# The centring of an expert layer's down weights, its first table and its weight loads moved into the recurrence of a fused kernel

## The chip, the cores and the metric

One NeuronCore of a Trainium2 chip runs the whole program. The metric is the time of one execution in microseconds; less is better. The engines are PE (TensorE), DVE (VectorE), ACT (ScalarE), POOL (GpSimd) and SP (SyncE), which here only issues DMAs. All data are fp32.

## What is computed

`x` is 16 sequences of 512 tokens of 128 channels. A gated delta rule over 16 heads of 8 channels is followed by a residual and a layernorm; then a mixture of 8 experts (top 1) with SiLU gating, again with residual and layernorm.

```python
def step(S, inp):                       # per head, over 512 tokens
    k_t, q_t, v_t, beta_t, a_t = inp
    S = S * a_t[..., None, None]
    delta = (v_t - einsum('bhd,bhde->bhe', k_t, S)) * beta_t
    S = S + k_t[..., :, None] * delta[..., None, :]
    return (S, einsum('bhd,bhde->bhe', q_t, S))
ctx = rmsnorm(ys, norm_w) * silu(gate)          # then ctx @ Wo.T + bo
x = layernorm(x + attn(x))
e = argmax(router(x))                            # one expert a token
out = down_w[e] @ (silu(gate_w[e] @ x) * (up_w[e] @ x))
x = layernorm(x + out)
```

## The kernel before

The 512 tokens of a sequence are cut into 16 blocks (`NW`) of 32 tokens, all 16 sequences at once; a block is eight chunks (`NCH`) of four tokens. A body function per engine (`pe_body`, `act_body`, `pool_body`, `dve_body`, `sp_body`) is called for block -1 (start-up), 0 to 15 and 16 (the tail), and each engine keeps the order in which its body writes the instructions. In block w the recurrence runs on block w, the projections are made for w+2 (`a`), the K products for w+1 (`n`), the outputs y for w-1 (`p`), residual, attention output and first layernorm for w-2 (`o`), the routing for w-3. Semaphores order the engines: `b.step` names an instruction, `b.wait` waits for it.

DVE's body is written by chunk: `chunk(c)` issues the product with the state (L1862), the decayed state (L1873), the reduction (L1878), the mix (L1882), its reduction (L1888), the update (L1892) and its reduction into the new state (L1904). Behind L1878, L1882, L1888, L1892 and L1904 stand five slots, `between(c, 0)` to `between(c, 4)`, in which other work of the block is put by hand: the routing steps (`route_part` 0 to 9), `y_next` (L1583), the eight `y_n` steps (L1555), `kkd`, `qkd`, `q_norm`. A slot is named (c, k) below. L1873 of chunk 0 waits for POOL's `solve3` of the block; the y of block w-1 is stored by SP after `y_n7`.

SP's body is a queue too. Per block: stores and loads of z, beta, v, x, q; then `x_res` (after PE's residual), the y store, the K store, the y load (after the y store has landed), the K load (after the K store has landed) and the Q load. K is written to HBM and read back in another layout; POOL's products of the next block start with it. POOL's body holds, in order, the eight products `q_prod` of a block, the products `kk` and `qk`, the decays, `ctx`, `k_gam`, `k_end`, `q_gam`, the `u` and `solve` steps, and the indirect DMAs that send finished rows to the sorted table (three a block from block 4 on).

In block 15 (`b.last`) the order differs: `last_between` places the steps; SP loads gate, up and down weights there. The first table (`table_a`, steps 0 to 15, on one partition) says which expert each of the first 29 tiles of 128 sorted rows takes; it needs the counts of the first nine blocks (`WA`). Its temporaries lie in a PSUM bank (`side`). Steps 0 to 10 are in block 15, the others in the tail (`last_outputs`), as are the memsets `pads` and the centring of the down weights: `centre_down` takes the mean of each of 24 rows of 128 out of `down_we` so that the output of the experts has no mean. The expert stage then takes 71 tiles through PE, ACT and DVE (`expert_pe`, `expert_act`, `expert_dve`), the first steps of which lie between PE's, ACT's and DVE's last attention work.

SBUF before: the attention's buffers (`sa`) lie first, and `gate_up_we`, `down_we`, `w_tile` and what follows are laid over them after `att.close()`.

## Time and profile before

| | |
|---|---|
| runs, us | 773.49, 773.37, 770.83 (median 773.37) |
| the profiled execution, us | 774.71, its span 772.9 |
| busy: PE, DVE, POOL, ACT | 84%, 82%, 78%, 54% of the span |
| mean granted clock of TensorE | 0.925 |
| start-up, until the first chunk | 26.5 us |
| blocks 0 to 15 | 26.5 to 568 us |
| tail and experts | 568 to 772.9 us |

Times in the rows are us from the span's start. A timeline row has the start, the duration, the engine, the line and the tiles written and read; a bracket gives the idle time before it and what ended it. A row with x3 stands for three instructions merged, its duration from the start of the first to the end of the last. Most instructions of POOL have the line of a helper (L1311) and are told apart by their tiles.

### The profile page before, as it was taken

To read this page: it belongs to the slowest core of one execution; us is meant where nothing else is said; L and a number is where in the kernel's file an instruction comes from. 1 tells how busy PE (TensorE), PEld (TensorE's weight loads), DVE (VectorE), ACT (ScalarE), POOL (GpSimd) and SP (SyncE) were. 2 spreads that over 40 slices of the span, in tenths; PEclk is the share of its full clock that TensorE was granted. 3 is DMA by queue.
4 is the path that set the end of the run, shared out by engine and by line. 5 is a ranking of instruction groups with operands and counts; after the bars stand their busy time and mean duration, and the time that the engine had idled before them with its cause. 6 is when DMAs were issued, how large, how long until landed. Compare 5 with 4: busy or idle time off the path is not lost.

```text
span 772.9 us, 13851 instructions
## 1 busy us (share of the span) xinstructions
PE 651.5 (84%) x3513; PEld 499.5 (65%) x3513; DVE 632.9 (82%) x1701; ACT 416.5 (54%) x1313; POOL 601.4 (78%) x758
## 2 busy tenths in 40 slices
PE   8668698889989887897988999496879979999990
PEld 3435374747657464664747556384778979999990
DVE  3899999999999999999999999999892535666530
ACT  6736456565565665566566546432324446666651
POOL 2888787979999899999999999999561527444574
PEclk9989799899999999999999999789669999999996
DMA  6734243341625334262433515304534655776730
GB/s 175 199 100 99 47 121 84 85 124 51 157 60 131 96 91 106 73 157 70 126 93 89 122 51 136 88 22 159 195 106 138 205 215 175 254 245 232 233 118 9
DMA packets 135919, 97.28 MB, mean 126 GB/s; under 512 B 95630, under 2 KB 110225, under 8 KB 135714
## 3 DMA queue, kind: packets, MB, share of 16 engines
q1 hardware_dynamic: 130514, 87.55, 40.2%
q0 software_dynamic: 4320, 8.43, 3.3%
q8 instruction: 30, 0.49, 0.3%
q10 hardware_dynamic: 1008, 0.43, 0.2%
q14 instruction: 47, 0.39, 0.2%
HBM read 39.80 MB, written 31.43 MB: 92 GB/s over the span
## 4 chain that ended last, share of the span: by engine, by line
PE 33%; DVE 31%; POOL 19%; issue 7%; ACT 6%; DMA 2%; ACTq 0%; DVEq 0%; POOLq 0%; SPq 0%
PE banks L436 12%; DVE banks L1904 6%; PE banks L449 6%; DVE banks L1878 5%; POOL q_prod L1311 5%; DVE upd L1892 5%; DVE prod L1862 4%; DVE banks L1888 3%; DVE mix L1882 3%; PE banks L695 3%; POOL u L1311 3%; DVE upd L1873 3%; PE banks L849 2%; PE banks L676 1%; POOL kkqk L1311 1%
## 5 line engine op out<-in xcount | busy, mean ns | idle before, releaser
L1311 POOL TENSOR_TENSOR q_prod<-s_keep,q_gam 128x512 f32<-128x512 f32 x128 | 140.5, 1099 | 15.8 <-ACT d_keep L1012 8.6
L1008 ACT ACTIVATE s_keep<-banks 128x128 f32<-128x128 f32 x128 | 50.2, 392 | 179.2 <-DVE upd L1892 177.2
L752 PE MATMUL banks<-q_prod,ident 128*128 128x240 f32 (+1 forms) x496 | 112.6, 381 | 24.6 <-POOL q_prod L1311 24.6
L752 PEld LDWEIGHTS banks<-q_prod,ident 128*128 128x128 f32 x496 | 93.9, 194 | 44.9 <-POOL q_prod L1311 35.0
L1904 DVE TENSOR_REDUCE banks<-upd 128x128 f32<-128x640 f32 x128 | 105.8, 826 | 7.7 <-DVE upd L1892 0.5
L436 PE MATMUL banks<-xs_t,w_tile 128*128 128x128 f32 x852 | 108.9, 278 | 3.6 <-issue 2.7
L545 POOL DMA_INDIRECT out<-rows_out,xs x71 | 70.0, 986 | 51.5 <-ACT rows_out L526 43.4
L436 PEld LDWEIGHTS banks<-xs_t,w_tile 128*128 128x128 f32 x852 | 102.3, 194 | 4.8 <-issue 4.4
L580 DVE TENSOR_TENSOR hid<-banks,silu 128x384 f32<-128x384 f32 x71 | 39.6, 557 | 72.9 <-PE banks L436 42.2
L1878 DVE TENSOR_REDUCE banks<-prod 128x64 f32<-128x576 f32 x128 | 93.6, 732 | 0.0
L1862 DVE TENSOR_TENSOR prod<-banks,k_gam 128x512 f32<-128x512 f32 x128 | 88.3, 690 | 3.4
L1892 DVE TENSOR_TENSOR upd<-banks,k_end 128x512 f32<-128x512 f32 x128 | 88.4, 690 | 1.9
L349 POOL DMA_INDIRECT x_sorted<-x_all,place x64 | 63.5, 993 | 17.6 <-issue 10.2
L695 PE MATMUL banks<-kkqk,ident 128*128 128x256 f32 (+1 forms) x272 | 64.0, 392 | 7.7 <-DVE qkd L1573 3.6
L676 PE MATMUL banks<-x_ct,w_proj 128*128 128x512 f32 x128 | 66.0, 640 | 2.8 <-DMA x_ct<-in_x_ct 2.8
L695 PEld LDWEIGHTS banks<-kkqk,ident 128*128 128x128 f32 x272 | 51.4, 202 | 18.4 <-issue 6.2
L449 PE MATMUL banks<-down_we,hid 128*128 x426 | 60.6, 279 | 0.5 <-issue 0.2
L1888 DVE TENSOR_REDUCE banks<-mix 128x64 f32<-128x256 f32 x128 | 54.4, 425 | 1.3
L449 PEld LDWEIGHTS banks<-down_we,hid 128*128 128x128 f32 x426 | 53.7, 194 | 1.6 <-issue 1.5
L1882 DVE TENSOR_TENSOR mix<-solve,banks 128x256 f32<-128x256 f32 x128 | 53.7, 419 | 1.0
L1873 DVE TENSOR_TENSOR upd<-banks,decays 128x128 f32<-128x128 f32 x128 | 48.9, 382 | 0.1
L950 PE MATMUL banks<-x_ct,ident 128*128 128x512 f32 x78 | 41.4, 671 | 8.1 <-DVE y_n L1555 8.1
(224 smaller groups left out, 1454.9 us busy)
## 6 DMA issues: line engine op xcount, KB each, us to landing
w_tile<-gate_up_we SPq DMA_DIRECT2D x71, 352.0 KB, 3.1
xs<-x_sorted SPq DMA_DIRECT2D x71, 64.5 KB, 2.2
x_ct<-in_x_ct SPq DMA_DIRECT2D x16, 256.0 KB, 3.0
k_dram<-kq_s SPq DMA_DIRECT2D x16, 256.0 KB, 2.9
q_dram<-kq_s SPq DMA_DIRECT2D x16, 256.0 KB, 3.9
out<-v_s SPq DMA_DIRECT2D x16, 256.0 KB, 2.6
out<-beta SPq DMA_DIRECT2D x16, 256.0 KB, 3.4
k_h<-k_dram SPq DMA_DIRECT2D x16, 256.0 KB, 3.2
```

Of the source, the lines that this page charges most:

```text
L436: last = mm(ps(tile)[:, c * P:(c + 1) * P], w_tile[tile % NG][:, g * I + c * P:g * I + (c + 1) * P], xs_t[tile % NX][:, :], start=True, st ...
L449: last = mm(down_ps[tile % 2][:, 0:D], hid[tile % NH][:, c * P:(c + 1) * P], down_we[:, c, :, :].rearrange("p e d -> p (e d)")[:, bass.ds( ...
L676: b.step(label, win, lambda: mm(by_slot(bank), w_proj[:, m, :], x, start=True, stop=True))
L695: i = mm(out[:, first:last], ident[:, :], kkqk[:, d, first:last], start=(d == 0), stop=(d == DH - 1))
L752: i = mm(out, ident[:, :], q_prod[m][:, d, :, 1 - m:], start=(m == 0 and d == 0), stop=(d == DH - 1), skip_group_check=True)
L1311: b.step(label, win, lambda: tt(out, x, y, op))
L1862: v.tensor_tensor(pr[:, :, 0:DH].rearrange("p (e b j) d -> p e b j d", e=DH, b=2), s_in.unsqueeze(3).to_broadcast(wide), k_gam[par][:, c, ...
L1878: v.tensor_reduce(k_s, pr, AX, ALU.add).then_inc(s_read, 1)
L1882: v.tensor_tensor(mix[:, :, :, :], solve[par][:, c, :, :, :], k_s.rearrange("p (n j) -> p n j", j=C).unsqueeze(2).to_broadcast([P, DH * 2, ...
L1888: v.tensor_reduce(delta, mix[:, :, :, :], AX, ALU.add).then_inc(s_delta, 1)
L1892: v.tensor_tensor(upd[:, :, 0:C].rearrange("p (e b d) j -> p e b d j", e=DH, b=2), delta.rearrange("p (e b) j -> p e b j", b=2).unsqueeze( ...
L1904: v.tensor_reduce(after[:, 0:P], upd[:, :, :], AX, ALU.add).then_inc(s_state, 1)
```

## The change

- `down_we` gets a place of its own in SBUF and is loaded in block 4. ACT centres it, three of the 24 rows of 128 a block, in blocks 6 to 13: one pass that sums the scaled row, one that adds the negative mean. DVE's `centre_down` goes.
- The sixteen steps of the first table go to eight slots each of blocks 13 and 14, and their temporaries (`tab`) from PSUM to SBUF.
- Gate and up weights are loaded in block 14, at its start on SP, instead of in block 15.
- In block 15 the routing steps 5 to 9 come in chunks 5 to 7 instead of 3 to 5; the memsets of the weight tiles come in (5, 3).
- In blocks 1 to 14 the `y_n` steps start in (4, 4) instead of (4, 3), and the last two are in (7, 1) and (7, 3) instead of (6, 3) and (7, 1).
- On ACT `q_squares` comes behind the first `keep` and `fill` of a block instead of ahead of them.
- The SBUF plan is changed so that the new places are free when they are written.

```diff
         fill_at = sb("fill_at", [1, E], I32)
+        tab = sb("tab", [1, 4 * E + TA * (E + 2)])
+        down_we = sb("down_we", [P, IC, E, D])
+        down_neg, down_sc = sb("down_neg", [P, IC * E]), sb("down_sc", [P, D])
 
 
...
-
+        v_h, k_gam, k_end, solve, q_gam = {}, {}, {}, {}, {}
+
+        def of_block(n):
...
+        v_h[1], v_h[2] = (sa(f"v_h{n}", [P, DH * 2 * C, NCH]) for n in (1, 2))
+        v_h[0] = sa("v_h0", [P, DH * 2 * C, NCH])
         a_h = two_a("a_h", [P, 2, C, NCH])
         z_h = sa("z_h", [P, 2 * T])
...
-        down_we = sb("down_we", [P, IC, E, D])
...
-        s_wpad, s_wmean, s_wdown = sem("s_wpad"), sem("s_wmean"), sem("s_wdown")
+        s_wpad, s_wdown = sem("s_wpad"), sem("s_wdown")
...
             v = nc.vector
-            at = 64
-            counts, shifted, whole, ends = (side[0:1, at + n * E:at + (n + 1) * E] for n in range(4))
-            past = side[0:1, at + 4 * E:at + 4 * E + TA * E].rearrange("p (s e) -> p s e", e=E)
-            row, expert_ps = (side[0:1, at + 4 * E + TA * (E + n):at + 4 * E + TA * (E + n + 1)] for n in range(2))
+            counts, shifted, whole, ends = (tab[:, n * E:(n + 1) * E] for n in range(4))
+            past = tab[:, 4 * E:4 * E + TA * E].rearrange("p (s e) -> p s e", e=E)
+            row, expert_ps = (tab[:, 4 * E + TA * (E + n):4 * E + TA * (E + n + 1)] for n in range(2))
...
-                    eng.wait_ge(s_wmean, 3)
+                    eng.wait_ge(act.sem, act.at["centred23", CENTRE + IC * E // 3 - 1])
...
-            for n in range(NG):
-                v.memset(w_tile[n][:, 2 * I:I + IC * P], 0.0).then_inc(s_wpad, 1)
...
                 b.step("logits", win, lambda: A(logits[:, at:at + TW, :],
                                                 post_of(win)[:, 0:TW * E].rearrange("p (i e) -> p i e", i=TW), ACT.Copy))
 
+            def centre_down(j):
+
+                n = 3 * (w - CENTRE) + j
+                if not 0 <= n < IC * E:
+                    return
+                block = down_we[:, :, :, :].rearrange("p c e d -> p (c e) d")[:, n, :]
+                if n == 0:
+                    b.wait_dma(s_wdown, 1)
+                b.step(f"mean{n}", w, lambda: A(down_sc[:, :], block, ACT.Copy, scale=-1.0 / D, accum_out=down_neg[:, n:n + 1]))
+                b.wait(act, f"mean{n}", w)
+                b.step(f"centred{n}", w, lambda: A(block, block, ACT.Identity, bias=down_neg[:, n:n + 1]))
+
             def start_up():
 
                 b.wait(pe, "k", 0)
...
                     nc.scalar.preload_act_table_set("natural_log_exp_and_others")
             if b.pre:
                 decay_of(n)
-                q_squares(n)
             keep(NCH * w)
             if b.chain:
                 fill(4 * w + 1)
+            if b.pre:
+                q_squares(n)
             if b.load:
                 b.wait(pe, "v", a)
                 b.wait_dma(s_vst, a)
...
                 fill(4 * w + 2)
+            centre_down(0)
             if b.post:
                 y_square()
             keep(NCH * w + 3)
...
+            centre_down(1)
             if b.load:
                 softplus(a)
             keep(NCH * w + 6)
             fill(4 * w + 4)
+            centre_down(2)
             if b.out:
                 router_logits(o)
 
...
+                places = ((0, 3), (1, 0), (1, 1), (1, 2), (2, 1), (2, 2), (3, 3), (3, 4))
+                if w in (NW - 3, NW - 2) and (c, k) in places:
+                    table_a_part(len(places) * (w - NW + 3) + places.index((c, k)))
...
                     kkd_part(k + 1)
-                if b.post and c == 4 and 3 <= k:
-                    if k == 3:
-                        b.wait(act, "y_r1", p)
-                    y_n_part(k - 3)
+                if b.post and c == 4 and k == 4:
+                    b.wait(act, "y_r1", p)
+                    y_n_part(0)
                 if b.post and c == 5 and k < 4:
-                    y_n_part(k + 2)
+                    y_n_part(k + 1)
                 if b.pre and c == 5 and k == 4:
                     q_norm_part()
                 if b.pre and c == 6 and k < 3:
                     qkd_part(k)
                 if b.post and c == 6 and k == 3:
-                    y_n_part(6)
-                if b.post and c == 7 and k == 1:
-                    y_n_part(7)
+                    y_n_part(5)
+                if b.post and c == 7 and k in (1, 3):
+                    y_n_part(6 + k // 2)
 
             def last_between(c, k):
 
@@ -1757,24 +1771,26 @@
                     y_next_part()
                 if c == 2 and k < 2:
                     route_part(r, 3 + k)
-                if c == 3 and k < 3:
-                    route_part(r, 5 + k)
                 if c == 3 and 3 <= k:
                     if k == 3:
                         b.wait(act, "y_r1", p)
                     y_n_part(k - 3)
                 if c == 4 and k < 3:
                     y_n_part(2 + 2 * k, 2)
-                if c == 4 and k == 4:
+                if c == 5 and k < 3:
+                    route_part(r, 5 + k)
+                if c == 6 and k == 4:
                     route_part(r, 8)
-                if c == 5 and k == 0:
+                if c == 7 and k == 0:
                     route_part(r, 9)
-                if c == 5 and 1 <= k:
-                    table_a_part(k - 1)
-                if c == 6:
-                    table_a_part(4 + k)
-                if c == 7 and k < 2:
-                    table_a_part(9 + k)
+                if c == 5 and k == 3:
+                    pad_weights()
+
+            def pad_weights():
+
+                if not b.dry:
+                    for n in range(NG):
+                        nc.vector.memset(w_tile[n][:, 2 * I:I + IC * P], 0.0).then_inc(s_wpad, 1)
 
             def table_a_part(k):
 
...
                     q_end[:, :, :].rearrange("p d b -> p b d").unsqueeze(1).to_broadcast([P, DH, 2, DH]), ALU.mult))
                 if not b.dry:
-                    for k in range(11, n_table_a):
...
                     y_ps[p % 2].rearrange("p (n t) -> p n t", t=T)[:, :, T - 1], ends, AX, ALU.add))
-                if not b.dry:
-                    for k in range(n_table_a, n_steps_a):
-                        table_a(e, k)
-                    centre_down(e)
...
                 e.dma_start(x_res[:, :], t["x_ct"][:, p, :]).then_inc(s_xres, 16)
-                b.wait(pool, "solve3", w)
-                b.wait(pe, "kkqk", w)
-                for s in (s_kst, s_qst, s_vst, s_bst, s_zst):
-                    b.wait_dma(s, NW)
-                e.dma_start(gate_up_we[:, :, 0, :], t["gate_w"]).then_inc(s_wexp, 16)
-                e.dma_start(gate_up_we[:, :, 1, :], t["up_w"]).then_inc(s_wexp, 16)
...
                 q_store(a)
+            if w == CENTRE - 2:
+                e.dma_start(down_we[:, :, :, :], t["down_w"]).then_inc(s_wdown, 16)
+            if w == NW - 2:
+                b.wait(act, "silu", NW - 1)
+                b.wait(pe, "warm", NW - 3)
+                b.wait(pool, "ctx", NW - 5)
+                b.wait(pool, "k_n", NW - 1)
+                e.wait_ge(s_kst, 16 * NW)
+                e.wait_ge(s_qst, 16 * NW)
+                e.wait_ge(s_vst, 16 * NW)
+                e.wait_ge(s_bst, 16 * NW)
+                e.wait_ge(s_zst, 16 * NW)
+                e.dma_start(gate_up_we[:, :, 0, :], t["gate_w"]).then_inc(s_wexp, 16)
+                e.dma_start(gate_up_we[:, :, 1, :], t["up_w"]).then_inc(s_wexp, 16)
             if b.post:
                 b.wait(pe, "res", o)
                 e.dma_start(x_res[:, :], t["x_ct"][:, p, :]).then_inc(s_xres, 16)
```

## Rows read from the trace of the kernel before

**Rows 1.** Busy time by stretch: span, engines (instructions), granted clock, DMA share, GB/s.
```profile
397.70:431.20 33.50, 30.11 (x134) 20.23 (x133) 32.67 (x83) 20.00 (x61) 31.91 (x43) 0.95 0.41 102
...
531.80:568.10 36.30, 26.48 (x120) 23.63 (x120) 33.41 (x83) 11.74 (x52) 24.36 (x25) 0.76 0.53 181
...
583.80:772.90 189.10, 164.73 (x1409) 160.88 (x1409) 87.38 (x336) 100.83 (x370) 93.52 (x96) 0.95 0.56 186
```

**Rows 2.** Waits of DVE, 60 to 560 us: total, times, longest.
```profile
DVE banks L1614 <- PE banks L839: 2.1, 1, 2.1
...
DVE y_n L1555 <- ACT y_rms L1039: 1.6, 1, 1.6
...
DVE banks L1904 <- ACT d_keep L1012: 0.3, 1, 0.3
```

**Rows 3.** Timeline of DVE, ends and starts of blocks: start, us, instruction [idle before].
```profile
294.62 0.21 DVE L1555 TENSOR_TENSOR y_n<-banks,y_rms 128x64 f32<-128x64 f32 x1
...
295.20 0.69 DVE L1892 TENSOR_TENSOR upd<-banks,k_end 128x512 f32<-128x512 f32 x1
...
296.92 0.69 DVE L1862 TENSOR_TENSOR prod<-banks,k_gam 128x512 f32<-128x512 f32 x1
297.72 0.39 DVE L1873 TENSOR_TENSOR upd<-banks,decays 128x128 f32<-128x128 f32 x1
...
330.64 0.69 DVE L1862 TENSOR_TENSOR prod<-banks,k_gam 128x512 f32<-128x512 f32 x1
331.25 0.38 DVE L1873 TENSOR_TENSOR upd<-banks,decays 128x128 f32<-128x128 f32 x1
```

**Rows 4.** Timelines of SP, POOL, DVE, blocks 10 and 11; landing of `k_h`.
```profile
395.61 0.34 SPq L1923 DMA_DIRECT2D out<-y_n  x1
...
398.99 0.33 SPq L1983 DMA_DIRECT2D k_h<-k_dram  x1
...
402.36 2.10 POOL L1311 TENSOR_TENSOR kkqk<-k_h 128x384 f32<-128x384 f32 x3 [0.64 <-DMA k_h<-k_dram]
...
428.90 2.11 POOL L1311 TENSOR_TENSOR solve<-u,b_h 128x384 f32<-128x384 f32 x3
...
431.19 0.69 DVE L1862 TENSOR_TENSOR prod<-banks,k_gam 128x512 f32<-128x512 f32 x1
...
DMA to landing us min/median/max: 2.6/3.2/4.2
```

**Rows 5.** Timeline of DVE in block 15, without and with a table step.
```profile
537.54 0.42 DVE L1882 TENSOR_TENSOR mix<-solve,banks 128x256 f32<-128x256 f32 x1
538.00 0.43 DVE L1888 TENSOR_REDUCE banks<-mix 128x64 f32<-128x256 f32 x1
...
560.87 0.42 DVE L1882 TENSOR_TENSOR mix<-solve,banks 128x256 f32<-128x256 f32 x1
561.21 0.39 DVE L274 TENSOR_TENSOR banks<-banks,iota_t 1x232 f32<-1x232 f32 x1
561.52 0.40 DVE L1888 TENSOR_REDUCE banks<-mix 128x64 f32<-128x256 f32 x1
```

**Rows 6.** A POOL product, instructions of the tile `k_gam`: min/median/max ns.
```profile
L1311 POOL TENSOR_TENSOR k_gam<-k_h,decays x16: 1267/1278/1303, 20.7 to 511.0; 128x512 f32<-128x512 f32 x16
```

**Rows 7.** Timelines of PE and SP in block 15, end of the residual.
```profile
551.44 1.91 PE L783 MATMUL banks<-center,x_res 128*128 128x128 f32 x8
...
553.38 0.33 SPq L2027 DMA_DIRECT2D x_res<-in_x_ct  x1
553.82 0.38 SPq L1923 DMA_DIRECT2D out<-y_n  x1
```

**Rows 8.** Timeline of ACT in block 7: a Square with accumulation, and the next.
```profile
285.53 0.27 ACT L1096 ACTIVATE post_sq<-banks 128x128 f32<-128x128 f32 x1
...
285.78 0.28 ACT L1096 ACTIVATE post_sq<-banks 128x128 f32<-128x128 f32 x1
```

**Rows 9.** Timeline of DVE in the tail: the last y product.
```profile
582.24 0.69 DVE L1820 TENSOR_TENSOR y_n<-banks,y_rms 128x512 f32<-128x512 f32 x1 [2.73 <-ACT y_rms L1039]
```

More of the change, by code:

```diff
@@ L122, in two_a @@
             return [sa(f"{name}{n}", shape) for n in range(2)]
+        spare = sa("spare", [P, 1480])
         x_ct = two_a("x_ct", [P, WN])
@@ L128, in block_kernel @@
         v_s = sa("v_s", [P, WN])
+        gate = {n: sa(f"gate{n}", [P, WN]) for n in (1, 2)}
         k_h = two_a("k_h", [P, DH, 2, C, NCH])
@@ L138, in block_kernel @@
         z_relu, z_log = sa("z_relu", [P, 2 * T]), sa("z_log", [P, 2 * T])
-        v_h = [sa(f"v_h{n}", [P, DH * 2 * C, NCH]) for n in range(3)]
         decays = two_a("decays", [P, 2, 9, NCH])
-        k_gam = two_a("k_gam", [P, NCH, 2, C, DH])
-        k_end = two_a("k_end", [P, NCH, 2, DH, C])
-        solve = two_a("solve", [P, NCH, DH * 2, C, C])
+        of_block(1)
         kkd = sa("kkd", [P, 96])
@@ L149, in block_kernel @@
         x_res = sa("x_res", [P, WN])
-        gate = [sa(f"gate{n}", [P, WN]) for n in range(5)]
-        q_gam = two_a("q_gam", [P, NCH, DH, 2, C])
+        gate.update({n: sa(f"gate{n}", [P, WN]) for n in (0, 3, 4)})
         q_norm = [sa(f"q_norm{n}", [P, 2 * T]) for n in range(3)]
@@ L205, in block_kernel @@
         tail_top, tail_place = (side[:, n:n + TW] for n in (SIDE + 2 * TW * E, SIDE + 2 * TW * E + TW))
-        down_mean = side[:, SIDE + 80:SIDE + 80 + IC * E]
         cand, before = (chain_ps[n][:, 2 * P:2 * P + TW * E].rearrange("p (t e) -> p t e", e=E) for n in range(2))
```

18 lines of the change are left out of this document (6 added, 12 removed).

## The prediction

> **What bounds the kernel now.** I read the table of stretches first, by block. A block is eight chunks of the recurrence, each starting with the DVE product of L1862. In a typical block DVE is busy 32.7 of 33.5 us, POOL 31.9, ACT only 20.0 [rows 1]; block 15 takes 36.3 to its end. DVE's order is the clock of the first 568 us: DVE's waits from block 1 to block 15 come down to three, of 2.1 us (block 15), 1.6 and 0.3 (both block 3), beside small change [rows 2]. So anything that adds to DVE's order, or makes DVE wait, is paid in full; work on ACT is not, as long as it comes before it is needed. After 583.8 us TensorE works through the experts: 164.7 us busy in 189.1 [rows 1].
>
> The second thing to see is how near POOL is to being the bound. At each block's start DVE's second instruction (L1873) needs POOL's last step for that block, `solve3`. Its natural place is 0.61 us after L1862, as in block 9; in block 8 it came 0.80 us after [rows 3], because POOL was late. POOL itself starts its block's real work when the reloaded K arrives: the `kkqk<-k_h` products waited 0.64 us for that DMA, and from their start (402.36) to the end of the solve products (428.90 + 2.11 = 431.01) POOL has no pause [rows 4]. DVE's next L1862 is at 431.19 [rows 4], so L1873 at 431.80; with about 0.1 us for the hand-over the slack is 431.80 - 0.1 - 431.01 = 0.69 us.
>
> **Part 1, the last `y_n` step goes from slot (7,1) to slot (7,3).** In block 7 it started at 294.62, behind the mix product; its new place is behind L1892, which starts at 295.20, and a step in that place starts 0.61 later, at 295.81 [rows 3]. It is 1.2 us later. This costs DVE nothing by itself, but the y store waits for it, and SP's queue behind that store is: K store, y load (waits for the y store to land), K load, Q load. The y store went out at 395.61, the K load at 398.99, and POOL's K products began at 402.36 [rows 4], each link waiting for the one before. So all move by 1.2 us, and POOL's solve ends 1.2 us later: against a slack of 0.69, DVE stalls 1.2 - 0.69 = 0.5 us. A stall in one block moves the next y store too, which gives the block after it as much slack back; so the loop runs over two blocks and loses its overhang once in two. The slack is not the same everywhere: block 7's K came later, and the solve there already cost block 8 0.80 - 0.61 = 0.2 us [rows 3]; there all of the 1.2 us, less what the loop has given back, is new. Blocks 4 to 13 have this full POOL load (before block 4 POOL sends no rows to the sorted table), so there are five loops. At 0.5 each they lose 2.5 us; I add 0.8 for the late K of block 7 (the 0.2 of block 8 shows that the slack there is used up, so 1.2 rather than 0.5 hits there, with a little of it still falling on the next): +3.3. Bounds: 0, if K lands as fast as the fastest one (2.6 us after its issue where the median is 3.2 [rows 4]), and 1.2 x 5 = 6.0.
>
> **Part 2, the table of the first part moves to blocks 13 and 14.** A short step in a slot between dependent DVE instructions is free: without one L1888 starts 0.46 us after L1882. The 1x232 steps are not: with L274 between them it is 0.65, so 0.19 [rows 5]. Five of the sixteen steps are of this size, 0.1 to 0.2 each: 0.8 us, which block 15 no longer pays and 13 and 14 now pay. In blocks 13 and 14 it is on the path: +0.8. In block 15 it is not, as part 3 shows.
> What no row shows is the price of such a step with both operands in SBUF. Before, `counts`, `ends`, `past` lay in PSUM; now `tab` is in SBUF, and seven steps (the subtraction, the scan, the compare, the product, two row sums, the last difference) read two SBUF tensors. POOL runs tensor products beside nearly all of chunks 0 to 3, the longest 1.3 us [rows 6]. Bounds for one step: below, its PSUM time (0 more; a gain is excluded, since the slot cannot become shorter than its dependent neighbours); above, 1.3 us, the longest POOL product it could have to wait out. I take 0.43, the mean rest of the POOL instruction that runs at that time (products of 0.2 to 1.3 us, descriptor work without a tensor left out): 7 x 0.43 = 3.0 us. The lower end has as little to support it: there is no row of a DVE step with two SBUF operands beside a POOL product. About 0.4 us of these delays fall before block 14's and 15's own loop stall and cover it, so part 1 gives 2.9 instead of 3.3.
> The Trainium skill says of this (SBUF — State Buffer, "Who interferes with whom") that a VectorE instruction with two SBUF inputs contends with a GpSimd instruction that reads SBUF, and that the second to issue blocks until the first is done. By that rule the wait is real and the sum is 779.4 us; with the rows' PSUM times alone it would be 776.8. No row here shows it.
>
> **Part 3, block 15.** The route step L1614 waited 2.09 us for PE's count [rows 2]; it moves two chunks on, where the count is long done, so the stall goes, and with the table gone (0.8) DVE ends its chain about 2.9 us sooner. What is late next: the last y store. It is issued at 553.82 behind SP's reload of `x_res` (553.38), and that waits for PE's residual, whose last group runs from 551.44 for 1.91 us [rows 7]. Earlier `y_n` steps thus help by 0.1 us at most, and everything behind (y load, ctx, attention, x1, `s_keep6`, `q_prod6`, the last y sums) hangs on the store. I book 0. PE was at 0.76 of full clock in block 15 [rows 1]: at full clock the residual would be early and up to 2.1 us would be real; that is a case of its own.
>
> **Part 4, ACT.** `q_squares` behind `s_keep0` and `fill`: in block 3 it held up `d_keep`, for which DVE waited 0.3 [rows 2]. `y_n0` one slot later: its wait for `y_rms` was 1.6 there, and the slot is 0.8 later, but K's 1.2 us delay reaches PE's lag sums and so `y_rms`. I book -0.6 (bounds -1.9, both waits gone, and +1.0). The 24 centring pairs: a Square with accumulation followed by its read takes 0.25 us of issue (285.53 to 285.78 [rows 8]), the second pass about the same, with the wait between 0.8 a pair, 2.4 us a block on an engine with 13 us free. They lie before `y_square`, before `softplus` and before `logits`, each over 1.5 us ahead of its reader: 0. If the cover were gone, 0.8 per pair.
>
> **Part 5, transfers and the end.** The down weights go out in block 4 behind `q_store`: some 3 us of SP issue in a stretch where SP then waits for PE's residual, 0. Gate and up weights in block 14: their waits are all for block 13 work; behind them on SP are `x_res` and a y store not due before the block's end, 0. In the tail DVE loses three table steps, the memsets and 7 us of centring, but the y product that follows had been idle 2.73 us waiting for `y_rms` [rows 9]; that wait grows. SP can load expert weights 9 us sooner, but its queue stands again at that same y store. So 0.
>
> **Sum.** 2.9 + 0.8 + 3.0 - 0.6 + 0 + 0 = +6.1 us. The profiled execution took 774.7 us (span 772.9), which gives 780.8; it is 1.3 above the median 773.4 of the runs shown, so for the median 779.4, rounded 779.0.
>
> **Rivals.**
> (a) The table steps cost what they did from PSUM: 3.3 + 0.8 - 0.6 = +3.5, 776.8 us. For it: none of these steps uses more than one partition.
> (b) Other side: the reload loop has slack after all. If K lands within about 2.6 us of its issue (the fastest in the trace) the loop costs nothing; then the stalls removed in block 3 (1.9) and, with PE at full clock, block 15 (2.1) count, against 0.8 for the table: 773.4 - 1.9 - 2.1 + 0.8 = 770.2. It decides at a slack of 1.2 us; measured 0.69.
> (c) As forecast, but TensorE keeps its full clock through block 15: 779.4 - 2.1 = 777.3. The clock fell there after PE had waited for `y_sq`; nothing in the change shortens that wait.
> (d) PE's clock falls in other blocks, because PE's wait for `y_n7` ahead of its warm-up products grows by 1.2 us; a block with this costs 1.6 as in block 3 [rows 2], two to three of them: 783.
> (e) A table load for the Identity pass, 1.3 us twice a pair: over 790. Nothing in the trace speaks for it.
>
> **How the numbers follow.** Forecast 0.45, (a) 0.25, (b) 0.12, (c) 0.09, (d) 0.08, (e) 0.01. The forecast's own range is 777 to 782. The whole range, 772.5 to 783.0, takes in (a), (c), (d) and the upper side of (b). Slower by over 0.5% means over 777.2: the forecast nearly whole, (d), (e), part of (a) and (c): 0.57. Within 0.5%, which is about what can be told from no change: 0.31. Faster 0.12.
>
> **What would show it.** L1873 of blocks 5 to 14 stands over 0.61 us behind L1862 in every second block, POOL's K products start about 5.8 us into the block instead of 4.7, and the y store goes 1.2 us later: part 1 right; otherwise (b). Table steps with start gaps of 1 us and more in chunks 1 to 3 of blocks 13 and 14: part 2 right, else (a). In block 15 no wait at L1614, yet the store directly behind `x_res`: part 3. A y product at the tail that waits over 9 us for `y_rms`: part 5. ACT as the releaser of a DVE wait in blocks 6 to 13 would prove part 4 wrong.

## The result and the profile after

| | before | after |
|---|---|---|
| median of the runs, us | 773.13 (4 runs) | 788.89 (4 runs, 785.92 to 789.26) |
| ratio, 95% interval | | 1.0196 [1.0172, 1.0219] |
| the profiled execution, us | 774.71, span 772.9 | 785.92, span 784.1 |
| mean granted clock | 0.925 | 0.914 |
| blocks 2, 3, 4 together | 102.8 | 104.1 |
| blocks 5 to 12 together | 268.3 | 270.8 |
| blocks 13 and 14 together | 67.1 | 72.0 |
| block 15 starts at | 531.8 | 540.9 |
| from there to the end | 241.1 | 243.2 |

Slower by 15.8 us in the medians; the forecast was 779.0. The two profiled executions differ by 11.2: 0.4 before the first chunk, 1.3 in blocks 2 to 4, 2.5 in 5 to 12, 5.0 in 13 and 14, 2.1 behind. The profiled execution of after is its fastest, 3.0 under its median, and that of before is 1.6 over its own; these 4.6 us stand in no trace, so no cause below accounts for them.

Busy time by stretch of after (columns as in [rows 1]): from the start of block 15, and the experts.

```profile
540.90:577.20 36.30, 24.20 (x107) 21.23 (x108) 31.62 (x77) 8.44 (x37) 21.80 (x23) 0.71 0.26 79
...
592.20:784.10 191.90, 168.33 (x1425) 164.70 (x1423) 88.57 (x341) 102.80 (x374) 93.58 (x96) 0.93 0.54 183
```

DVE's work in block 15 fell from 33.4 to 31.6 us [rows 1], and so did PE's, from 26.5 to 24.2: PE gets through less of its order in the same 36.3 us. The expert stage itself did not get longer: from the first expert tile's product to the end it is 188.2 us before and 187.8 after. The waits of DVE, 60 to 575 us (columns as in [rows 2]):

```profile
DVE upd L1883 <- POOL solve L1323: 2.0, 5, 0.5
DVE kkd L1573 <- PE banks L691: 1.4, 1, 1.4
DVE y_n L1567 <- ACT y_rms L1035: 1.4, 3, 0.7
```

The wait for the count is gone (2.1 in [rows 2]), and `solve` is a new name. The reload loop, timelines of SP, POOL and DVE, blocks 10 and 11, which answer to [rows 4]:

```profile
400.19 0.34 SPq L1933 DMA_DIRECT2D out<-y_n  x1
...
403.58 0.33 SPq L1993 DMA_DIRECT2D k_h<-k_dram  x1
...
407.18 2.10 POOL L1323 TENSOR_TENSOR kkqk<-k_h 128x384 f32<-128x384 f32 x3 [0.52 <-DMA k_h<-k_dram]
...
433.73 2.11 POOL L1323 TENSOR_TENSOR solve<-u,b_h 128x384 f32<-128x384 f32 x3
...
402.30 0.39 DVE L1883 TENSOR_TENSOR upd<-banks,decays 128x128 f32<-128x128 f32 x1 [0.54 <-POOL solve L1323]
```

Block 11 starts at 401.07, so the K load goes out 2.5 us into the block and POOL's products start 6.1 into it; before it was 398.99 - 397.7 = 1.3 and 4.7. The solve ends at 435.84, and block 12 starts at 435.20; before it ended 0.2 ahead of the next block. The last row is DVE's stall at the start of block 11. Block 13 of after, DVE and POOL, two steps of the table beside POOL's products:

```profile
479.72 1.15 POOL L1323 TENSOR_TENSOR kkqk<-q_h,k_h 128x256 f32<-128x256 f32 x2
480.82 1.11 POOL L1323 TENSOR_TENSOR q_prod<-s_keep,q_gam 128x512 f32<-128x512 f32 x1
...
480.44 0.45 DVE L281 TENSOR_TENSOR_SCAN tab<-ones,tab 1x8 f32<-1x8 f32 x1
481.14 1.04 DVE L283 TENSOR_TENSOR tab<-tab,iota_t 1x232 f32<-1x232 f32 x1
```

The scan ends at 480.89, as POOL's `kkqk` does (480.87); the compare ends at 482.18, 0.25 behind `q_prod` (481.93). From PSUM the compare took 0.39 [rows 5].

Block 15 of after, timelines of PE, DVE and SP, which answer to [rows 7]:

```profile
556.98 1.85 PE L822 MATMUL banks<-w_r,x_ct 128*128 128x8 f32 x8
564.27 2.04 PE L776 MATMUL banks<-bias_o,ident 128*128 128x512 f32 x2 [5.44 <-DVE end_at L1630]
566.10 1.91 PE L779 MATMUL banks<-center,x_res 128*128 128x128 f32 x8
...
563.96 0.16 DVE L1630 TENSOR_TENSOR end_at<-banks,end_at 128x8 f32<-128x8 f32 x1
...
568.05 0.33 SPq L2030 DMA_DIRECT2D x_res<-in_x_ct  x1
568.48 0.38 SPq L1933 DMA_DIRECT2D out<-y_n  x1
```

PE stands still for 5.44 us and starts the residual 0.15 behind the end of the routing step `ends` (L1630: the residual overwrites the bank that this step reads, and the program makes `residual` wait for it). The y store follows 27.6 us into the block; before it was 22.0 (553.82 - 531.78).

### The profile page after: what moved, and what is told of

The parts are those of the page before. It is cut to its first block and busy times, and to the rows that moved or that the text cites. A ratio compares the mean times of both kernels' runs of the same rounds, so it can differ in the third digit from the quotient of the medians.

```text
span 784.1 us, 13921 instructions
## 1 busy us (share of the span) xinstructions
PE 654.8 (84%) x3513; PEld 506.0 (65%) x3513; DVE 629.1 (80%) x1698; ACT 434.1 (55%) x1385; POOL 601.9 (77%) x758
## 5 line engine op out<-in xcount | busy, mean ns | idle before, releaser
L748 PE MATMUL banks<-q_prod,ident 128*128 128x240 f32 (+1 forms) x496 | 116.2, 390 | 20.2 <-POOL q_prod L1323 20.2
L748 PEld LDWEIGHTS banks<-q_prod,ident 128*128 128x128 f32 x496 | 97.2, 200 | 42.1 <-POOL q_prod L1323 30.0
L445 PE MATMUL banks<-xs_t,w_tile 128*128 128x128 f32 x852 | 110.9, 282 | 1.2 <-ACT silu L486 0.9
L554 POOL DMA_INDIRECT out<-rows_out,xs x71 | 70.0, 986 | 52.9 <-ACT rows_out L535 45.4
L445 PEld LDWEIGHTS banks<-xs_t,w_tile 128*128 128x128 f32 x852 | 104.3, 197 | 2.3 <-issue 1.9
L946 PE MATMUL banks<-x_ct,ident 128*128 128x512 f32 x78 | 46.0, 736 | 26.0 <-DVE y_n L1567 26.0
L946 PEld LDWEIGHTS banks<-x_ct,ident 128*128 128x128 f32 x78 | 16.8, 230 | 55.9 <-issue 55.9
```

The source lines that it names most:

```text
L445: last = mm(ps(tile)[:, c * P:(c + 1) * P], w_tile[tile % NG][:, g * I + c * P:g * I + (c + 1) * P], xs_t[tile % NX][:, :], start=True, st ...
L554: eng.indirect_dma_start(t["out"], bass.IndirectOffsetOnAxis(ap=xs[tile % NR][:, D:D + 1].bitcast(I32), axis=0), rows_out[tile % NO][:, :] ...
L748: i = mm(out, ident[:, :], q_prod[m][:, d, :, 1 - m:], start=(m == 0 and d == 0), stop=(d == DH - 1), skip_group_check=True)
```

## The experiments

Kernels on one chip are compared with the kernel before on that chip. "a_" starts from the changed kernel, "b_" from the one before, "c_" takes back several parts. The two times are medians; the ratio is an estimate over all runs of both and can differ from that of the medians (by 0.3% in a_table15), and us that follow from it are given by the ratio. No "a_" kernel had the changed kernel beside it; where they are set against it, it is after_again, from another comparison.

| kernel | before there, us | this, us | ratio, 95% interval |
|---|---|---|---|
| b_route_moved | 787.96 | 794.43 | 1.0068 [1.0043, 1.0093] |
| a_route_back | 787.96 | 796.37 | 1.0093 [1.0062, 1.0125] |
| a_table15 | 787.96 | 799.51 | 1.0113 [1.0054, 1.0172] |
| a_yn_back | 787.96 | 797.38 | 1.0111 [1.0069, 1.0152] |
| after_again | 790.39 | 801.57 | 1.0148 [1.0121, 1.0175] |
| c_three_back | 790.39 | 792.29 | 1.0024 [1.0005, 1.0042] |
| c_three_back_warm | 790.39 | 789.89 | 0.9990 [0.9970, 1.0009] |
| b_warm15 | 790.39 | 787.50 | 0.9969 [0.9950, 0.9987] |
| b_table_early | 788.25 | 791.97 | 1.0044 [1.0022, 1.0067] |
| b_yn_late | 788.25 | 789.88 | 1.0020 [0.9997, 1.0043] |
| c_no_centre | 788.25 | 787.86 | 0.9995 [0.9974, 1.0016] |
| b_warm_more | 788.25 | 785.36 | 0.9950 [0.9930, 0.9970] |
| c_three_again | 773.09 | 773.04 | 1.0000 [0.9972, 1.0027] |
| c_no_centre_again | 773.09 | 771.48 | 0.9977 [0.9949, 1.0005] |
| c_qsq_back | 773.09 | 772.81 | 0.9989 [0.9960, 1.0017] |
| b_warm_qsq | 773.09 | 770.03 | 0.9969 [0.9943, 0.9995] |

### The routing steps of block 15

The new theory: not the count but `ends`, two chunks later, holds PE's residual and with it x_res and the y store. The rival: the later store is a matter of PE's clock. b_route_moved makes that edit alone. a_route_back puts steps 5 to 7 of the changed kernel back in chunk 3 (`c == 3 and k < 3`); 8 and 9 stay late there.

```diff
-                if c == 3 and k < 3:
-                    route_part(r, 5 + k)
+                if c == 5 and k < 3:
+                    route_part(r, 5 + k)
-                if c == 4 and k == 4:
+                if c == 6 and k == 4:
                     route_part(r, 8)
-                if c == 5 and k == 0:
+                if c == 7 and k == 0:
                     route_part(r, 9)
```

> The kernel before with nothing changed but block 15's routing steps: 5 to 7 in chunk 5, 8 and 9 in chunks 6 and 7. Theory: PE's residual waits for `ends`, the y store leaves 5 us later, +2 to +5.6 us although DVE's 2.1 us wait is gone. Rival (my recorded part 3, the store does not move): 0, within 0.5.

> The changed kernel with routing steps 5 to 7 of block 15 back in chunk 3. Theory (PE's residual of block 15 waits for routing step 6, `ends`, which now comes two chunks later): the idle time of 5.4 us ahead of PE's residual goes, the last y store of block 15 leaves 22 us into the block instead of 27.6, the 2.1 us wait of DVE at routing step 5 comes back, and the time falls by 2 to 5.6 us. Rival (block 15 and the tail are set by TensorE's clock, not by this wait): less than 1 us.

Timelines of PE, b_route_moved first, then a_route_back, and SP's y store in each:

```profile
557.53 2.05 PE L780 MATMUL banks<-bias_o,ident 128*128 128x512 f32 x2 [8.74 <-DVE end_at L1618]
...
561.74 0.38 SPq L1923 DMA_DIRECT2D out<-y_n  x1
```
```profile
555.38 1.85 PE L822 MATMUL banks<-w_r,x_ct 128*128 128x8 f32 x8
557.08 2.06 PE L776 MATMUL banks<-bias_o,ident 128*128 128x512 f32 x2
...
561.30 0.38 SPq L1933 DMA_DIRECT2D out<-y_n  x1
```

With the edit alone the residual waits 8.74 us for `ends` and starts 23.4 us into the block, the store goes out at 27.6, and the whole is 0.68% longer, 5.4 us, as expected. With the three steps back there is no idle time ahead of the residual (16.7 us into the block), the store is at 20.9 and the first expert tile's product 51.7 us into the block, where after_again (below, from another comparison, as slow as this one) has it at 57.8. Of the 2.1 us stall for the count, expected back, 1.0 came. The stall that the move removed is real, and the end gains nothing from it. The rival falls: the granted clock over these 36.3 us is 0.74 in both, and the store differs by 6.7 us. All kernels of the study say the same: in the five with the late steps the store goes out at 27.6 us and the first expert product comes at 55.4 to 61.0; in the thirteen others at 19.6 to 22.0 and 48.7 to 53.2.

### The table

a_table15 puts the steps of the changed kernel back in block 15 and the tail (the last five now in one run), with `tab` still in SBUF; b_table_early puts the steps and `tab` of the kernel before where the change has them, and nothing else:

```diff
+        tab = sb("tab", [1, 4 * E + TA * (E + 2)])
-            at = 64
-            counts, shifted, whole, ends = (side[0:1, at + n * E:at + (n + 1) * E] for n in range(4))
+            counts, shifted, whole, ends = (tab[:, n * E:(n + 1) * E] for n in range(4))
...
+                places = ((0, 3), (1, 0), (1, 1), (1, 2), (2, 1), (2, 2), (3, 3), (3, 4))
+                if w in (NW - 3, NW - 2) and (c, k) in places:
+                    table_a_part(len(places) * (w - NW + 3) + places.index((c, k)))
...
-                if c == 5 and 1 <= k:
-                    table_a_part(k - 1)
```

> The changed kernel with the table's sixteen steps back in block 15 and the tail, their temporaries still in SBUF. Theory (a step with SBUF operands waits for POOL's running instruction): blocks 13 and 14 fall from 36.2 and 35.9 us to 33.5 to 34.2, the time by 4 to 5 us if block 15 has the room; in block 15 the steps that meet an idle POOL take their old 0.15 to 0.39 us and those beside a POOL product more. Rival (the slots themselves cost, 0.8 us for five wide steps): -0.8 us, and the steps are as long in block 15 as in 13 and 14.

> The kernel before with the table's sixteen steps alone in blocks 13 and 14 and their temporaries in SBUF. Theory (the steps wait for POOL's products, and DVE's chain pays that in full): blocks 13 and 14 take 36 to 38 us each in place of 33.5, their steps 0.3 to 2 us each; block 15 keeps its wait for the count of some 2 us and its late residual, so nothing comes back there; in all 4 to 6 us longer than before. Rival (the steps cost their own execution of 0.15 us alone, and the long blocks 13 and 14 of the changed kernel are the work of its later loop): both blocks at most 34.2, the whole within 1.5 us of before.

In a_table15 blocks 13 and 14 are back at 33.8 and 34.0 us. The whole gained less than the 4 to 5 us expected (1.0113, after_again 1.0148), and the first expert product came later than in after_again, 61.0 us into the block against 57.8. The same steps with the same SBUF operands cost nothing extra while POOL has no product: timelines of DVE and POOL in block 15 and the tail of a_table15.

```profile
565.82 0.15 DVE L281 TENSOR_TENSOR_SCAN tab<-ones,tab 1x8 f32<-1x8 f32 x1
566.28 0.38 DVE L283 TENSOR_TENSOR tab<-tab,iota_t 1x232 f32<-1x232 f32 x1
...
581.27 1.70 DVE L301 TENSOR_SCALAR capped<-tab 1x8 f32<-1x8 f32 x1
...
572.86 1.26 POOL L1323 TENSOR_TENSOR ctx_t<-y_ch,gate 128x512 f32<-128x512 f32 x1 [9.43 <-DMA y_ch<-out]
...
581.82 1.11 POOL L1323 TENSOR_TENSOR q_prod<-s_keep,q_gam 128x512 f32<-128x512 f32 x1
```

Scan and compare, with POOL idle, take 0.15 and 0.38, within a hundredth of what they took from PSUM. The step that met a product in the tail took 1.70 and ended at 582.97, 0.04 behind it; it had started 0.55 ahead of the product, and why it did not end first is not shown. b_table_early makes blocks 13 and 14 35.8 and 36.6 us, +5.4 together; the whole is +3.5 (788.25 x 0.0044; 1.7 to 5.3), under the 4 to 6 expected. Some of the 5.4 may come back behind block 14; where is not shown. The rival (0.15 us each, both blocks at most 34.2) falls.

Of steps with their temporaries in PSUM beside a product of POOL the kernel before has a case, in block 15 (timelines of POOL and DVE, the compare of [rows 5] behind them):

```profile
560.49 1.26 POOL L1311 TENSOR_TENSOR ctx_t<-y_ch,gate 128x512 f32<-128x512 f32 x1 [2.32 <-DMA y_ch<-out]
...
560.75 0.16 DVE L272 TENSOR_TENSOR_SCAN banks<-ones,banks 1x8 f32<-1x8 f32 x1
```

The product runs to 561.75; the scan (to 560.91) and the compare (561.21 to 561.60) run beside it in 0.16 and 0.39. The same kind of product does meet the SBUF operands in after: `ctx_t` at 481.87, which starts 0.31 before the compare ends, took 1.44 us, its fifteen other rows 1.26 to 1.29. So the operands' place decides, as far as these rows go; the early steps with their temporaries in PSUM were not tried.

### The y_n slots

```diff
-                if b.post and c == 4 and 3 <= k:
-                    if k == 3:
-                        b.wait(act, "y_r1", p)
-                    y_n_part(k - 3)
+                if b.post and c == 4 and k == 4:
+                    b.wait(act, "y_r1", p)
+                    y_n_part(0)
...
-                if b.post and c == 7 and k == 1:
-                    y_n_part(7)
+                if b.post and c == 7 and k in (1, 3):
+                    y_n_part(6 + k // 2)
```

b_yn_late makes this edit alone, a_yn_back takes it out of the changed kernel.

> The kernel before with the new slots of the y_n steps alone. Theory (reload loop: y store 1.2 us later, K load 1.2 later, POOL's solve 1.2 later, overhang lost once in two blocks): y store near 32.6 us into a block, POOL's K products near 6 us, several blocks from 4 to 14 at 33.8 to 34.3 where they were 33.5, in all 2.5 to 4 us longer than before. Rival (there is slack): all blocks stay at 33.5, within 1 us of before.

> The changed kernel with the eight `y_n` steps of a block in their old slots. Theory (y store, K store, K load and POOL's solve form a loop with too little slack): the y store leaves 31.4 us into a block instead of 32.6, POOL's K products start near 4.7 instead of 6.0, the stalls of 0.3 to 0.8 us at the start of blocks 5 to 12 go, and the time falls by 2.5 to 4 us. Rival (these stalls come from somewhere else, the centring on ACT for one): the stalls stay, less than 1 us.

In a_yn_back blocks 5 to 12 are all 33.50 to 33.55 us: the loop's stalls are gone. Together these eight take 270.8 to 271.5 us in the four kernels with the whole change's late slots (after, after_again, a_route_back, a_table15) and 268.1 to 269.4 in the thirteen with the old ones. Blocks 13 and 14 got longer (38.6 and 36.5, 8.0 over the kernel before): with K earlier, POOL's products lie back to back under the table's slots. Timelines of DVE and POOL in block 13 of a_yn_back:

```profile
468.60 2.21 DVE L275 TENSOR_TENSOR tiles_i<-tab,region_at 1x8 int32<-1x8 f32 x1
...
475.91 1.18 DVE L281 TENSOR_TENSOR_SCAN tab<-ones,tab 1x8 f32<-1x8 f32 x1
...
477.33 1.20 DVE L283 TENSOR_TENSOR tab<-tab,iota_t 1x232 f32<-1x232 f32 x1
...
467.41 2.10 POOL L1323 TENSOR_TENSOR kkqk<-k_h 128x384 f32<-128x384 f32 x3
469.48 1.09 POOL L1323 TENSOR_TENSOR q_prod<-s_keep,q_gam 128x512 f32<-128x512 f32 x1
...
475.79 1.27 POOL L1323 TENSOR_TENSOR k_gam<-k_h,decays 128x512 f32<-128x512 f32 x1
477.01 1.28 POOL L1323 TENSOR_TENSOR k_end<-k_h,decays 128x512 f32<-128x512 f32 x1
```

The scan ends 0.03 behind `k_gam` (477.06); the compare 0.24 behind `k_end` (478.29). The step at 468.60 ended at 470.81, 0.24 behind `q_prod`: it waited out the end of `kkqk` and the whole product after it. So the loop's delay hides part of the table's cost, and the two don't simply add: blocks 5 to 14 take 343.4 us here and 342.8 in after, and the 2.5 to 4 us that were expected back are not seen in them.

b_yn_late alone: store at 32.7 us, K load at 2.5, as expected, and K products at 5.2 to 6.1, mostly sooner than the 6 expected; blocks 4 to 14 lost 1.0 us, less than the 2.5 expected, and the interval of the whole (-0.2 to +3.4 us) takes in no loss at all. Blocks 5 to 12 take 269.1 us, within the range of the old slots, so alone the edit's cost is not told from noise. One difference is in the landing of `k_h` (its tile's instructions, b_yn_late, then after):

```profile
DMA to landing us min/median/max: 2.5/2.7/4.1
```
```profile
DMA to landing us min/median/max: 2.8/3.4/4.0
```

K landed 0.7 us sooner than in after (medians). Why is not shown: in the others it was 3.0 to 3.5, whatever the slots.

### What is left when the three are taken back

after_again is the changed kernel, again; c_three_back has the three edits out (the temporaries in PSUM again). What stays in it: the centring on ACT, the early loads, `q_squares` behind the first keep, the SBUF plan, and in block 15 the late steps 8 and 9 and the early memsets.

> The changed kernel once more, on the chip of the following three. Expected 1.020 of the kernel before, as first measured; in the trace the three causes as in its first trace: stalls behind POOL's solve in blocks 5 to 12, table steps of up to 1.0 us in blocks 13 and 14, 5.4 us of PE idle before the residual of block 15.

> The changed kernel with three things back as they were: routing steps 5 to 7 of block 15 in chunk 3, the table in block 15 and the tail with its temporaries in PSUM, the `y_n` steps in their old slots. What is left of the change: centring on ACT, the earlier weight loads, `q_squares` behind the first `keep` and `fill`, the memory plan. Theory (the three causes are all of the loss): 1.000 of the kernel before, within 0.003. Rival (the centring on ACT or the loads cost something too): 1.005 or more.

after_again was 1.0148 of the kernel before where 1.020 was expected; the first pair's 1.0196 was not reached again, and why is open. The three account for nearly all of the 1.0148: it becomes 1.0024 on one chip, and the single edits add to 0.68 + 0.44 + 0.20 = 1.32%. Two parts of what is left were taken apart, once more beside it on one chip: c_no_centre and c_no_centre_again (one kernel) leave the centring out, so that the experts' output keeps its mean (their first down product waits for the load of `down_we` in its place), c_three_again is c_three_back, and c_qsq_back has `q_squares` in its old place.

```diff
-                b.step(f"mean{n}", w, lambda: A(down_sc[:, :], block, ACT.Copy, scale=-1.0 / D, accum_out=down_neg[:, n:n + 1]))
...
+                return
```
```diff
+                q_squares(n)
             keep(NCH * w)
             if b.chain:
                 fill(4 * w + 1)
-            if b.pre:
-                q_squares(n)
```

> The kernel with route, table and y_n taken back, and without ACT's centring passes too: it leaves the centring of the down weights out, so the experts' output keeps its mean. Theory (centring on ACT is covered): within 1 us of the kernel with three back, that is 1 to 3 us over before. Rival (the passes hold something up): blocks 2 to 4 or 6 to 13 shorter, and the whole at the time of before or under it.

> The kernel with route, table and y_n taken back once more, beside its variants on one chip. If what is left of the change (ACT's order and centring, earlier loads, memory plan) costs the 1 to 3 us measured before: ratio to before 1.001 to 1.004. If that was the chip's: 0.998 to 1.001.

> As c_no_centre (the centring of the down weights is left out, so the experts' output keeps its mean). If the 24 pairs of centring passes on ACT cost something: 1.5 to 3 us under the kernel with three back. If they are covered, as the prediction booked: within 0.8 us of it.

> The kernel with three back and q_squares ahead of the first keep again, its old place. If the new place is worth something (the prediction's part 4): block 3 longer by 1 to 3 us and the whole by as much. If it costs: start-up 0.3 us sooner, block 3 no longer, the whole shorter.

On the last chip what is left costs nothing (c_three_again 1.0000), and without centring it is 1.6 us less, with overlapping intervals. The centring showed in no wait: c_three_back has it, and its DVE waits for neither ACT nor POOL from 60 to 560 us, blocks 5 to 12 taking 268.1 us against 268.3 before. In the whole it may cost up to about 2 us or nothing; this is open, and so is the place of `q_squares`: c_qsq_back was 2.0 us longer in block 3 than c_three_again (36.07 against 34.06) but the medians differ by 0.2. In all seven kernels with the old place block 3 takes 35.0 to 36.7 us; with the new place it takes 33.9 to 34.9 in six and 35.6 to 36.7 in five, the changed kernel's first profile among them. So the new place seems able to shorten it, and what decides is not shown.

### PE's clock in block 15

With the end of the chain hanging on PE in block 15, I gave PE something to do while it waits for `y_sq`: three `mm` calls, six MATMUL records, whose results nobody reads. b_warm15 and c_three_back_warm do this; b_warm_more adds seven calls further on, and b_warm_qsq is b_warm_more with the new place of `q_squares`.

```diff
                 b.wait(dve, "qkd2", w)
+                b.wait(act, "y_sq", w - 2)
+                b.wait(dve, "y_n7", w - 2)
+
+                def keep_warm():
+                    for _ in range(3):
+                        i = mm(y_ps[w % 2], ident[:, :], w_proj[:, 0:4, :], start=True, stop=True, skip_group_check=True)
+                    return i
+                b.step("warm", w, keep_warm)
                 y_sums(p, pre_ps[:, 2, 0:2 * T])
```

> The kernel c_three_back with six more matmuls in block 15 between the attention of block 13 and the y sums, where TensorE waited 2.9 us for `y_sq`. Theory (the last y store waits for PE's residual, which runs at half clock after that wait): the granted clock of block 15 goes from 0.76 towards 0.95, the residual ends 3 to 5 us sooner, the y store with it, and 2 to 5 us are gained against c_three_back. Rival (the store is bound elsewhere, or the clock falls a little later): within 0.5 us.

> The kernel before with the same six matmuls in block 15 and nothing else. Theory: as for c_three_back_warm, 2 to 5 us faster than the kernel before, 0.994 to 0.997. Rival: no difference.

> The kernel before with extra products on PE in three places of block 15 (ahead of the y sums, behind the first y sums, behind the late y sums), their results unused. Theory (PE's clock falls because PE stands still while it waits for y_sq and again later, and the end hangs on PE from there): the clock stays up through block 15 up to the first expert, the y store is near 20.5 us into the block in place of 22, s_keep6 and the first expert's product come 1 us or more sooner than with the first place alone, the whole 3 to 5 us under before. Rival (the products stand in the way of the attention they are put beside): no better than the first place alone, which was 2.4 under before, or over before.

> The kernel before with the extra products on PE in three places of block 15 and q_squares behind the first keep. If both gains add: block 3 some 34 to 35 us in place of 36, the whole 4 to 6 us under before. If the order of ACT brings nothing: 2.9 us under before, as the extra products alone gave.

PE in block 15 of b_warm_more:

```profile
541.65 2.74 PE L883 MATMUL banks<-w_proj,ident 128*128 128x512 f32 x6
544.23 1.89 PE L849 MATMUL banks<-y_sq,ident 128*128 128x64 f32 x16
...
546.77 1.04 PE L839 MATMUL banks<-one_hot,ones 128*128 128x32 f32 x8
```

The eight count products took 1.85 us before and 1.04 here. Two us of this stretch by window, b_warm_more, then the kernel before (columns as in [rows 1]):

```profile
546.20:548.20 2.00, 1.74 (x17) 1.65 (x17) 1.42 (x5) 1.60 (x6) 0.94 (x1) 1.00 0.93 384
```
```profile
546.00:548.00 2.00, 2.00 (x12) 2.00 (x11) 0.00 (x0) 0.91 (x4) 1.69 (x2) 0.50 0.56 226
```

The granted clock is 1.00 (2.4 GHz) here and was 0.50 (1.2 GHz) before; by 549.5 it is 0.50 in b_warm_more too. But these two us do not show what the extra products did. Three kernels without them (c_three_back, b_yn_late, b_route_moved) ran the count at 1.04 us as well. Timeline and window of c_three_back, where PE waited only 0.59 us for `y_sq` (2.87 in the kernel before):

```profile
539.27 1.97 PE L846 MATMUL banks<-y_sq,ident 128*128 128x64 f32 x16 [0.59 <-ACT y_sq L1027]
...
542.59 1.04 PE L836 MATMUL banks<-one_hot,ones 128*128 128x32 f32 x8
```
```profile
542.60:544.60 2.00, 1.95 (x19) 1.86 (x17) 2.00 (x7) 1.03 (x4) 1.57 (x2) 1.00 0.04 8
```

What sets the four kernels with extra products apart is the clock over the first 36.3 us of the block: 0.81 to 0.95, against 0.69 to 0.78 in the fourteen without. DVE's stall for the count is 0.8 us in b_warm15 and 0.6 in b_warm_more, but without extra products it is also anything from nothing to 2.1. The y store goes out at 20.5 to 20.6 us in b_warm15, b_warm_more and c_three_back_warm (19.6 in b_warm_qsq), within the 19.6 to 22.0 of the kernels with neither extra products nor late routing steps. The first expert product comes 53.2 us into the block in b_warm15 and 48.7 in b_warm_more, against 50.4 to 53.2 in those.

By the times, c_three_back_warm is 2.4 us under c_three_back (medians), as expected, and b_warm15 2.4 under the kernel before (0.9969). b_warm_more is 3.9 us under it (0.9950; the medians differ by 2.9) where 3 to 5 were expected, and b_warm_qsq 2.4 (0.9969) where 4 to 6 were, with block 3 at 36.1 us and not the 34 to 35 expected; so the order on ACT adds nothing that can be seen. That extra products help is shown by these intervals; that they help through the clock fits the higher clock of block 15, but the rows of a single profile do not show where the time was gained.

## Why the prediction was wrong

It had the sign and too small a size: 779.0 against 788.9, outside 772.5 to 783.0. (Its terms give 773.4 + 6.1 = 779.5; the last line has 779.0. This changes nothing.) Of the 15.8 us the profiled pair shows 11.2, of which 8.7 lie in blocks 2 to 14, where 6.1 were booked, 0.4 in the start-up and 2.1 behind block 14, where 0 was booked; 4.6 stand in no trace.

**The bound** (DVE's order in the recurrence, POOL close behind): right, and the losses of blocks 2 to 14 came through it.

**Part 1, the reload loop:** right in mechanism, and in size for the whole change. Booked 2.9; blocks 5 to 12 of after lost 2.5 us, and block 13 shows a stall for `solve` too (0.5). That the slots cause this is shown by a_yn_back, which has no such stall. Alone, with K 0.7 us sooner, blocks 4 to 14 lost 1.0; that the landing makes the difference is not shown.

**Part 2, the table:** right in mechanism, mis-sized. Booked 0.8 + 3.0; blocks 13 and 14 lost 5.0, of which 0.5 is the loop: 4.5 for 3.8. Alone, with POOL's products back to back, it was 5.4. The sum came out nearer than its terms. Seven steps were counted at 0.43 over their PSUM time, 3.0; in after these seven took 2.0 us longer than before. Four others, booked at nothing, took 2.0 longer too. The two errors pull against each other, which is luck. The term that failed is the count of steps: those with two tensors in SBUF were counted, but the copy (L273, 0.74), the scalar operations (L277 0.43, L289 0.47, L301 0.89) and in other kernels the casts (0.77 to 0.96) took longer as well, where all took 0.14 to 0.18 before, and only the reductions never did. And 1.3 was taken as the most for one step; in after the longest took 1.04, in a_yn_back one took 2.21. The Trainium skill (SBUF — State Buffer, "Who interferes with whom") says that copies, casts and scalar operations in a two-port mode contend with GpSimd too, and that the second to issue blocks for the whole instruction. The traces agree that these steps took longer beside POOL's products, with these numbers; in which mode they ran no run shows, and the step of 2.21, which outlasted a product that started 0.88 behind it, goes beyond the rest of one instruction. The prediction had the blocking from this section, but of what contends only the sentence on two inputs. The kernel before had the counter-case for its question, a PSUM step beside a product (above), and the prediction had not looked at POOL there. Rival (a), the steps at their PSUM price, falls.

**Part 3, block 15:** the step that failed, 0 booked for the routing steps' move. It let the stall for the count go and looked for what is late next on SP: the y store behind `x_res` behind the residual, which is right. It took the residual's time as given, since PE came late to it from work before it. But the residual also waits for the routing step `ends`, and this is one of the steps moved two chunks on. Before, `ends` was done at 548.67, 0.9 us ahead of the residual (549.59), so the wait showed in no row. Booked 0; by itself the edit costs 5.4 us. In the profiled pair 5.6 us at the y store became 2.5 at the first expert product (52.9 to 55.4 us into the block) and 2.1 at the end. Of what came back two places are seen: the attention's products, 2.08 us before and 1.16 after, and the y products of `y1_6` (3.67 and 2.00), which met a higher clock. The rest, to the 5.4 of the single edit, is not seen in this pair. The prediction's "booked 0" held one chain and left out who waits for the instructions that move.

**Part 4, ACT:** open. Booked -0.6; blocks 2 to 4 lost 1.3 in the profiled pair, with three waits for `y_rms` and one for PE (1.4, block 3) in place of the 1.6. But these three blocks take 100.9 to 105.9 us over the eleven kernels with the new place of `q_squares` (102.8 to 104.0 over the seven with the old), so neither sign nor size can be read from one pair. The prediction's own sign against it, ACT as the releaser of a DVE wait in blocks 6 to 13, did come once: 0.7 us for `gate` in block 9, at the first decayed state, where the stalls for `solve` stand. It does not convict the centring: a_yn_back and c_three_back have the centring and no such wait, while a_route_back, with the late y_n slots, has it too (block 7). So it goes with the loop.

**Part 5:** DVE's y product of the tail waited 9.87 us for `y_rms`, over 9 as forecast. The start-up was 0.4 longer, booked at 0; it runs from 26.3 to 27.2 us over the kernels, so this is no more than their spread. That the loads cost nothing fits c_three_again (1.0000); no kernel moved them alone.

**Rivals (b) to (e):** (b) falls, the loop has no slack. (c) and (d) rested on the clock; in block 15 it was 0.71, so (c) did not happen, and (d) was not seen as such: of DVE's waits for `y_rms`, 1.4 us in all, none lies outside blocks 2 to 4. (e) never showed. **The range** was missed for one reason that the runs show: no case had a price for an unseen waiter in block 15, 5.4 us by itself, and with it the sum passes 783.0. A second share is between executions: the pair that was profiled differs by 11.2 us, the medians by 15.8, and measured again the kernel was 1.0148 and not 1.0196 of the one before.

## What to carry to other kernels

When an instruction moves later, list everyone who waits for it, not only what it waited for: a wait that is met shows in no row, even when it is met by less than 1 us, and the move can turn it into the bound. A removed stall in an order like DVE's is worth nothing while the chain that ends the stage runs through another engine. Small steps put into a full DVE order cost little in a stretch where POOL has no product, and perhaps with operands outside SBUF (not tried in these slots); else book the rest of POOL's product for each, and at times the next one too. And before a row is taken as the work of an edit, look whether kernels without the edit have it too: the clock in block 15 comes both ways in kernels that do not touch it.

## What was not expected of the hardware

- A DVE step of eight numbers on one partition took up to 2.21 us with its operands in SBUF, beside POOL's products, and 0.15 where POOL had no product. It can wait out more than one product when they lie back to back. Copies, casts and scalar operations took longer too (0.43 to 0.96, and 1.70 once); reductions took 0.37 to 0.38 in every case.
- The kernel before took 773.1 us in two of the comparisons and 788.0 to 790.4 in the three others. Most of this lies in the expert stage: from the first expert tile's product to the end it is 187.2 to 188.2 us in the profiles of the first two and 200.8 to 204.6 in the others, while a block took the same 33.5. Why is not shown: two comparisons with the same chip number in the record have 788.25 and 773.09. So only kernels measured together are compared.
- Three `mm` calls whose results nobody reads, 2.7 us of PE's time, made the kernel 2.4 us shorter (0.9969 [0.9950, 0.9987]), with a granted clock of 0.83 over block 15 in place of 0.76.
- PE's clock over the same work of block 15 is not the same from kernel to kernel: in three kernels without extra products PE stood still for 0.4 to 0.7 us ahead of the `y_sq` products, and the eight count products behind them ran in 1.04 us; in the eleven others it stood for 0.9 to 2.9 us, and they took 1.85.
